# Weighted pairs are kept slot by slot instead of window by window: short runs when they are stored, whole rows when they are loaded

## The reference, cut to what matters

```python
    h = jnp.maximum(_layernorm(x, axis=-1), 0.0)
    x = x + _L2_gnn_ref(h, edge_index, edge_weight, L2_gnn_W, L2_gnn_b)
...
        dst = edge_index[0]
        src = edge_index[1]
        msgs = edge_values[:, None] * X[src]
        AX = jax.ops.segment_sum(msgs, dst, num_segments=X.shape[0])
        return jnp.einsum('nd,od->no', AX, W) + b
```

## Time and profile before

| | us |
|---|---|
| median of 3 runs | 5627.88 (5624.51 to 5636.4) |
| the profiled execution, its own time | 5615.62 |
| its span | 5614.0 |
| PE busy in the span | 4809.8 (86%) |
| VectorE busy | 3803.6 (68%) |
| ScalarE busy | 2156.4 (38%) |
| GpSimd busy | 2084.1 (37%) |
| mean rate of the DMA engines | 206 GB/s, 1154.88 MB in 1256468 packets |

### The profile page before, as it was taken

How to read it: one execution, slowest core, us unless ns; L and a number is a source line. 1 busy time by engine, 2 the same in 40 slices (tenths; PEclk the granted TensorE clock), 3 DMA queues, 4 the chain that set the end, 5 groups by cost and what they waited for, 6 DMA issues and landing times.

```text
span 5614.0 us, 102733 instructions
## 1 busy us (share of the span) xinstructions
PE 4809.8 (86%) x38297; PEld 3472.2 (62%) x38297; DVE 3803.6 (68%) x6119; ACT 2156.4 (38%) x3962; POOL 2084.1 (37%) x2152
## 2 busy tenths in 40 slices
PE   1299999948989888889888988859999998689997
PEld 0276666626777777777777777535555543456665
DVE  4888888757777777777777777479999976420001
ACT  0166666545555555555555555422222200000001
POOL 4122210007777777777777777200000000001110
PEclk6699999979999999999999999979999999699998
DMA  7256665427777777777777877649999999156664
GB/s 217 70 183 208 209 204 197 165 104 199 219 218 217 216 215 213 214 208 218 211 214 207 217 205 217 177 141 293 286 291 290 289 276 252 53 185 206 203 204 119
DMA packets 1256468, 1154.88 MB, mean 206 GB/s; under 512 B 468015, under 2 KB 1149860, under 8 KB 1207060
## 3 DMA queue, kind: packets, MB, share of 16 engines
q1 hardware_dynamic: 1129992, 802.56, 49.2%
q0 software_dynamic: 87488, 151.98, 11.8%
q10 hardware_dynamic: 38495, 193.76, 9.9%
HBM read 691.89 MB, written 468.81 MB: 207 GB/s over the span
## 4 chain that ended last, share of the span: by engine, by line
PE 47%; SPq 21%; DVE 9%; POOL 9%; issue 7%; DMA 4%; ACT 1%; DVEq 0%; POOLq 0%; ACTq 0%
PE psum L1385 46%; SPq L624 5%; POOL G L835 4%; SPq L627 4%; POOL H L835 4%; DVE R L858 4%; SPq L621 3%; DMA H<-local_dst_pairs 3%; SPq L632 2%; SPq L505 2%; DVE H L858 1%; SPq L483 1%; SPq L613 1%; DVE ACC L858 1%; POOL R L786 1%
## 5 line engine op out<-in xcount | busy, mean ns | idle before, releaser
L1385 PE MATMUL psum<-R,HT 128*128 128x384 bf16 x6076 | 1084.2, 326 | 59.8 <-DVEq L1374 59.8
L1703 ACT ACTIVATE HT<-psum 98x512 f32<-98x512 f32 (+2 forms) x1527 | 978.9, 679 | 381.6 <-PE psum L1385 307.9
L1385 PE MATMUL psum<-R 128*128 128x98 bf16 (+3 forms) x6858 | 982.6, 281 | 70.1 <-DVE R L858 27.7
L1703 ACT ACTIVATE H<-psum 128x512 f32<-128x512 f32 (+1 forms) x752 | 446.7, 597 | 1508.3 <-PE psum L1607 796.4
L835 POOL DMA_INDIRECT G<-gather_table,cols_pc x908 | 867.8, 956 | 420.0 <-issue 270.7
L835 POOL DMA_INDIRECT H<-gather_table,cols_pc x896 | 856.3, 956 | 295.0 <-issue 264.9
L1385 PEld LDWEIGHTS psum<-R,HT 128*128 128x128 bf16 x6076 | 566.7, 97 | 383.6 <-DVEq L1374 60.1
L1385 PE MATMUL psum<-R,ACC 128*98 128x128 bf16 x10752 | 784.6, 222 | 0.0
L1385 PEld LDWEIGHTS psum<-R,ACC 128*98 128x98 bf16 x10752 | 746.8, 126 | 0.2
L858 DVE TENSOR_TENSOR HT<-HT,psum 128x512 f32<-128x512 f32 (+1 forms) x949 | 607.6, 653 | 153.1 <-PE psum L1385 149.5
L1385 PEld LDWEIGHTS psum<-R 128*128 128x128 bf16 (+1 forms) x6858 | 568.8, 111 | 226.0 <-issue 36.8
(11 more groups left out here) (237 smaller groups left out, 5947.2 us busy)
## 6 DMA issues: line engine op xcount, KB each, us to landing
weighted_blocks<-HT ACTq DMA_DIRECT2D x224, 784.0 KB
adjacency_blocks<-HT SPq DMA_DIRECT2D x74, 1568.0 KB, 5.7
ACC<-weighted_blocks SPq DMA_DIRECT2D x74, 1568.0 KB, 12.9
R<-weighted_blocks SPq DMA_DIRECT2D x74, 1568.0 KB, 12.4
HT<-adjacency_blocks SPq DMA_DIRECT2D x50, 1568.0 KB, 6.5
H<-local_dst_pairs SPq DMA_DIRECT2D x113, 512.0 KB
weighted_blocks<-H SPq DMA_DIRECT2D x72, 784.0 KB
R<-attr_parts SPq DMA_DIRECT2D x451, 99.0 KB
```

Source lines behind the costliest of these rows:

```text
L1385: return nc.tensor.matmul(o, lhs_t, rhs, start=start, stop=stop)
L1703: return nc.scalar.activation(o, a, f, **kw)
```

## The change

`bw_d` becomes [block, 64 slots, 98 rows, 128 columns]. The stores write the same 784 KB of a group from the same buffers, but a row's 16 slots now go to 16 places, 512 bytes each. The load of a block becomes one transfer of 128 rows of 25088 bytes (the 98 rows x 128 columns of a slot are two partitions' rows, one after the other), so the semaphore of a load counts 16 instead of 32, and the counts in layer 3 that go on from it are adapted. No engine computes anything else, and no instruction moves past another.

```diff
-    bw_d = dram("weighted_blocks", [NBK, J, 64, P], f32)
+    bw_d = dram("weighted_blocks", [NBK, 64, J, P], f32)
...
-                sp.dma_start(bw_d[c // 4][:, HB * (c % 4):HB * (c % 4 + 1)],
+                sp.dma_start(bw_d[c // 4][HB * (c % 4):HB * (c % 4 + 1)].rearrange("q m c -> m q c"),
                              o.rearrange("m (q c) -> m q c", c=P)).then_inc(s_bst[c % 3], 16)
...
-                for d in range(2):
-                    sp.dma_start(BW_load[i % 2][d:P:2, :].rearrange("q (w c) -> q w c", c=P),
-                                 bw_d[i][d * W:(d + 1) * W].rearrange("w q c -> q w c")).then_inc(s_al[i % 2], 16)
+                sp.dma_start(BW_load[i % 2], bw_d[i].rearrange("q (d w) c -> (q d) (w c)", d=2)).then_inc(s_al[i % 2], 16)
...
-                    t.wait_ge(s_al[b % 2], 32 * (b // 2 + 1))
+                    t.wait_ge(s_al[b % 2], 16 * (b // 2 + 1))
...
-                    t.wait_ge(s_al[b % 3], 16 * (NBK * (b % 3 < 2) + b // 3 + 1))
+                    t.wait_ge(s_al[b % 3], 16 * (NBK // 2 * (b % 3 < 2) + b // 3 + 1))
...
-                act.dma_start(bw_d[c // 4][:, HB * (c % 4):HB * (c % 4 + 1)],
+                act.dma_start(bw_d[c // 4][HB * (c % 4):HB * (c % 4 + 1)].rearrange("q m c -> m q c"),
                               staged[c % 3].rearrange("m (q c) -> m q c", c=P)).then_inc(s_bst[c % 3], 16)
```

## The result

The changed kernel takes 5548.66 us (median of 3 runs, 5536.54 to 5554.38) against 5627.88: ratio 0.9858, 95% interval 0.9831 to 0.9885. It is 79 us faster. The forecast was 5720, slower by 92. The time lies within the range (5535 to 5815), which was drawn wide enough for rival B; the direction is wrong, and the forecast's own stretch (5640 to 5830) doesn't hold it. The profiled executions differ less than the medians: 5554.38 against 5615.62 us, -61.2. The table accounts for these; the 18 us more between the medians stand in no stage of it.

What follows compares the result with a forecast made beforehand. Attention was taken to be held by three full DMA engines through SyncE's issues. Stores +144 us, layer 2's main part -14 and tail -38 gave +92 us on 5627.9, so 5720 us; range 5535 to 5815.

Steps and rivals of the forecast that it cites:

- rival B: Attention stores: 512-byte runs are free, so only layer 2's gains act: -52 us, 5576 us; chance 12%.
- Step (a): Attention: ScalarE's 224 stores in 512-byte packets cost three full DMA engines 0.64 us more each, +144 us.
- (b): Attention: ScalarE's issue of stores with more runs grows by up to 60 us, covered by a copy: 0 on path.
- (c): Layer 2: SyncE's 72 late stores take 2.8 us instead of 2.15, cost 0 while the queue has room.
- (d): Layer 2's main part: block loads become 128 long rows, one issue; DMA share falls to about 0.75, -14 us.
- (e): Layer 2's tail: loads land in 8.8 us, within a block's 10.76; gaps vanish and clock rises: -38 us.
- A: Attention: 8-KB packets starve SyncE, so short ones let its pieces through: -106 us, 5522 us; chance 23%.
- C: Attention: a store's descriptors hold up SyncE's issues, 2.5 us a store, 570 us, 6146 us in total; chance 6%.
- D: Layer 2: whole rows bring nothing, leaving only the stores' 144 us, 5772 us; chance 6%.

Runs made afterwards that it cites:

- e1: Changed kernel with 128 bytes of gap after each 512-byte row, so blocks load in 512-byte runs again: 6193.87 us, 1.0056 of the kernel before.
- e13: Changed kernel, three of four gathers a step from step 8, each ScalarE store made twice, the second one step later: 6028.12 us, attention 2787.8.
- e14: Kernel before, three of four gathers a step from step 8, each ScalarE store made twice, the second one step later: 6083.55 us, attention 2793.6.
- e11: Changed kernel, three of four gathers a step from step 8, one more 256-byte DMA of SyncE in each step: 5858.59 us, attention 2629.5.
- e12: Changed kernel, three of four gathers a step from step 8, ScalarE's stores cut to one of 98 rows: 5214.85 us, attention 1973.3.
- e18: Changed kernel, all gathers, extras and attribute parts loaded over more DMA engines: 5518.08 us, 0.9833 of the kernel before, attention 2273.7.
- e7: Changed kernel, three of four gathers a step from step 8, extras and attribute parts loaded over more DMA engines: 5396.16 us, 0.9623, attention 2160.0.
- e5: Changed kernel with three of four gathers a step from step 8 of attention: 5551.34 us, attention 2308.6.
- e6: Kernel before with three of four gathers a step from step 8 of attention: 5593.45 us, attention 2297.1.
- e9: Changed kernel, three of four gathers a step from step 8, each ScalarE store made twice in a row: 6086.32 us, attention 2844.5.
- e10: Kernel before, three of four gathers a step from step 8, each ScalarE store made twice in a row: 6299.31 us, attention 3014.3.
- e0: Changed kernel unaltered, run again on a slower kind of chip: 6100.25 us against 6160.71 for the kernel before, 0.9904; attention 2859.7.

## Why the prediction was wrong

**Step (a), the full engines, failed.** The sum of 1888 of 1800 us was taken as proof that three engines are full, and then 0.64 us more per store as path. The same sum for the changed kernel: L627 351 x 99 x 47 ns / 3 = 544, the rest of q1 (10080 - 1633) / 16 = 528, q0 355, q10 7891 / 14 = 564, together 1991 of 1800 us, 111%, and no time was lost. A sum that can be 105% or 111% at the same pace doesn't tell whether an engine has room. Since the sums pass 100%, the times that the records give to packets must overlap in part. I had noticed it ("packets of two queues overlap a little") and passed over it; layer 2's share of 1.01 stood in the same table, and e1 has 1.06 over all 16 engines.

**The size of a store failed with it.** 28.6 ns a packet times 112 gives 3.20 us, and 6278 us of q10 gives 2.56; both are shares in the records, and both recur (7891 / 14 / 176 = 3.20). The price in time is 2.14 and 2.22 us by e13 and e14 (19.1 ns a 512-byte packet), and by the pairs on one chip the same for both forms, where step (a) had 0.64 us more for the short one. For the 8-KB store the prediction had that number at hand as a bound, 2.15 us for seven packets alone; for the short one its lowest bound was 2.88. That bound too was made of shares. A bound from the bytes moved would have reached below: 0.71 MB in 2 us at 356 GB/s is 802816 bytes in 2.26 us.

**That SyncE's row sets the pace was right** for the kind of chip on which it was made (e11: +321 us for one small issue a step; e12: -335 and then PE), and so was GpSimd close behind it (e18: -38 us until it is the bound; I had up to 54). What I added to it, that the row is slow because of three engines, isn't shown: e7's gain is covered by shorter issues. Whether the engines' backlog has a part in it stays open, and so does why one form of L624 is issued in 0.93 us and the other in 0.36. That a store does hold the row is clear from e12 and e13, and e5 against e6 and e13 against e14 show that it does so equally in both forms.

**(b) and (c)** cost nothing, as forecast. ScalarE's issue didn't grow at all (0.315 us, allowed for: 0.58), so no cover was needed. SyncE's late stores became cheaper to issue (5.48 to 0.42 us, medians), and ScalarE's waits for their landing fell from 85.4 to 44.4 us; I had them at no gain, and ScalarE isn't the bound there.

**(d) and (e)** held: -55.7 for -52. The main part gave 22.6 instead of 14, the tail 33 instead of 38. The landing was taken from a store of such rows, 8.8 us; the load takes 10.5 alone (median, tail) and 11.2 beside late stores, and the DMA share is 0.83, not 0.75. I had said that above 11 us step (e) would be wrong, and that at 10.8 it would give 20: in the tail, where it counts, it is 10.5, under a block's 10.76, and PE's idle time fell by 26 us there. That margin is 0.3 us, against 2 in the forecast: the tail came out near the forecast with less room than it had assumed. The clock rose to 0.99 (forecast 1.00).

**The rivals.** B (512-byte runs are free, 5576 us) is what happened: nothing in attention, whole rows in layer 2. 5554.38 in the profiled run is 61.2 below before; B's sum was 52. I gave it 12% against 53% because the shares spoke against it. A's mechanism (8-KB packets hold SyncE's short ones) exists, but costs time only with two stores in a row (e9 against e10: 170 us). C's 570 us fell: SyncE's DMA issues in attention did not become longer (L621 at most 3.1 us, before 3.4; L624 and L627 at most 2.0 and 1.8, before 3.1 and 2.4). A small part of its mechanism may be there: short runs lengthen SyncE's register reads (46 us in all), and the shorter issues give 54 back, so that two effects cancel. Why, no run shows. D fell with e1. The pairs for the exchange of single stores, changed minus before, are -10.1 (first kind) and +11.5 us (e5 against e6), and with twice the stores -5.8 (e13 against e14), so it is worth nothing within some 12 us.

## What to carry to other kernels

Look first whether the chain on the chip at hand goes through the engine that you price: on the second kind here PE hid what SyncE's row costs. Busy shares of DMA queues may not be added up to a verdict that an engine is full, nor their growth taken as time: price a transfer by doubling it where it lies on the path. Where an engine's own row of DMA issues carries the chain, count issues and their durations first; one small DMA a step cost 0.71 us, and another order of two loads' dimensions saved 0.46 of issues. Whichever side of a transfer is on the path should have the long rows: here the loads of layer 2 gained 56 us and the stores lost nothing with 512-byte runs.

## What the runs showed of the hardware that I had not expected

- Two stores of 8-KB packets in a row cost 3.20 us for the second, apart 2.22; with 512-byte runs 2.39 and 2.14 (e9, e10, e13, e14, counted from e5 and e6).
- Short-run stores lengthen SyncE's register reads instead of its issues: L505 takes 2.32 us (median) instead of 1.41, and 4.12 with two stores in a row (e9).
- Issuing 98 x 16 runs takes ScalarE as long as 98 (0.315 and 0.314 us), but a second such store right behind holds it for 2.16 us (e9), with 8-KB packets 0.41 (e10).
- A DMA of SyncE of 256 bytes was issued in 0.53 us, longer than L621's 64 KB in 0.345 (e11).
- 128 rows of 25088 bytes land in 10.5 us as a load (tail) and in 8.8 as a store.
- Chips differ: on some, PE halts between the products that build blocks, 424 us in all with no releaser in the trace (e0; 0.0 on others), and attention takes 2860 instead of 2311 us, with layer 2 the same to a microsecond. With a fourth of the gathers left out the halts there are 25 us (e5). The cause is open.
